# Half steps in lockstep, 128-column pieces of maxima and masks off TensorE in the two 16-head attentions

## What is computed

```python
# l2a: heads of 8 features, strict mask: masked scores are 0, not -inf
att = einsum('bhqe,bhke->bhqk', q, k) / sqrt(8)
att = softmax(att * tril(ones, k=-1), axis=-1)
out = einsum('bhqk,bhke->bhqe', att, v)          # then out @ Wr + br
# l2r: heads of 4 features, rotated q and k, causal mask
c = rmsnorm(x) @ w_down                          # 64 latents
q, k, v = rope(c @ wq), rope(c @ wk), c @ wv
scores = where(causal, q k^T / sqrt(4), -inf)
x = x + (softmax(scores) @ v) @ w_up
```

## Time and profile before

| | us |
|---|---|
| median of three runs (4970.01 to 4974.94) | 4973.66 |
| the profiled execution | 4970.81 |
| its span, first to last instruction | 4969.1 |
| PE busy | 3646.9 (73%) |
| DVE busy | 2768.8 (56%) |
| ACT busy | 1422.5 (29%) |
| POOL busy | 727.7 (15%) |
| mean granted TensorE clock, share of 2.4 GHz | 0.794 |

### The profile page before, as it was taken

How to read it: one execution, slowest core, us unless ns; L and a number is a source line. 1 busy time by engine, 2 the same in 40 slices (tenths; PEclk the granted TensorE clock), 3 DMA queues, 4 the chain that set the end, 5 groups by cost and what they waited for, 6 DMA issues and landing times. The chain is left out here.

```text
span 4969.1 us, 75102 instructions
## 1 busy us (share of the span) xinstructions
PE 3646.9 (73%) x29138; PEld 2469.8 (50%) x29138; DVE 2768.8 (56%) x7107; ACT 1422.5 (29%) x2785; POOL 727.7 (15%) x465
## 2 busy tenths in 40 slices
PE   4577887887548788778654878878865487887885
PEld 4354654455435455445443545544545355554454
DVE  6674544456576454445757655444575765444457
ACT  3033332320304333232130433323213133332320
POOL 2142200000114220000012332000001233200000
PEclk6588987898558888799755888878975598897897
DMA  1000000000000000000000000000000000000000
GB/s 25 5 19 19 1 2 2 12 16 1 6 11 13 19 1 2 2 11 17 1 6 23 1 19 1 2 1 11 17 1 6 23 1 19 1 2 1 11 17 5
DMA packets 55964, 43.16 MB, mean 9 GB/s; under 512 B 14451, under 2 KB 52262, under 8 KB 55590
## 3 DMA queue, kind: packets, MB, share of 16 engines
q1 hardware_dynamic: 54358, 37.53, 2.6%
q10 hardware_dynamic: 1232, 0.61, 0.1%
HBM read 35.50 MB, written 2.10 MB: 8 GB/s over the span
## 5 line engine op out<-in xcount | busy, mean ns | idle before, releaser
L157 POOL TENSOR_TENSOR ln_rstd<-ln_var_eps,neghalf 128x4 f32<-128x4 f32 x128 | 129.8, 1015 | 2199.2 <-DVE ln_var_eps L169 2199.1
L1906 DVE TENSOR_REDUCE l2r_m<-l2r_bank_ring 128x1 f32<-128x384 f32 (+3 forms) x352 | 207.2, 637 | 259.8 <-PE l2r_bank_ring L1755 259.8
L1906 DVE TENSOR_REDUCE l2a_m<-l2a_bank_ring 128x1 f32<-128x384 f32 (+3 forms) x352 | 207.2, 637 | 247.5 <-PE l2a_bank_ring L1755 247.5
L1137 POOL TENSOR_TENSOR l1t_ss<-l1t_ss,neghalf 128x16 f32<-128x16 f32 x64 | 240.4, 3756 | 460.0 <-DVE l1t_ss L1192 460.0
L2020 ACT ACTIVATE l2r_P<-l2r_bank_score 128x512 f32<-128x512 f32 x320 | 168.6, 594 | 284.7 <-PE l2r_bank_score L1782 156.5
L2020 ACT ACTIVATE l2a_P<-l2a_bank_score 128x512 f32<-128x512 f32 x320 | 169.3, 597 | 268.3 <-PE l2a_bank_score L1782 140.0
L1381 PE MATMUL l1t_ring<-l1f_qkv,x_normT 128*128 128x512 f32 x384 | 226.8, 741 | 13.5 <-ACT x_normT L1046 13.5
L1746 PE MATMUL l2r_bank_ring<-l2r_k_head,l2r_q_head 32*128 32x256 f32 (+3 forms) x1024 | 184.2, 540 | 33.5 <-DVE l2r_m L1906 26.8
L1465 PE MATMUL l1t_score<-l1t_q_head,l1t_k 128*128 128x256 f32 (+1 forms) x896 | 207.2, 363 | 0.0
L1746 PE MATMUL l2a_bank_ring<-l2a_k_head,l2a_q_head 32*128 32x256 f32 (+3 forms) x1024 | 176.6, 516 | 25.8 <-DVE l2a_m L1906 21.8
L1346 ACT ACTIVATE l1t_P<-l1t_score 128x512 f32<-128x512 f32 x176 | 105.2, 598 | 222.9 <-PE l1t_score L1465 222.9
(11 more groups left out here) (561 smaller groups left out, 8483.2 us busy)
## 6 DMA issues: line engine op xcount, KB each, us to landing
l2e_w<-in_L_ffn_w SPq DMA_DIRECT2D x96, 128.0 KB, 2.2
l1f_qkv<-in_L_ffn_wqkv SPq DMA_DIRECT2D x8, 768.0 KB, 4.3
l1f_tables<-in_l_tables SPq DMA_DIRECT2D x8, 512.0 KB, 5.9
l1f_w<-in_L_ffn_w SPq DMA_DIRECT2D x8, 341.0 KB
x_in<-in_L_attn_hidden_states SPq DMA_DIRECT2D x10, 256.0 KB, 3.5
l1f_wo<-in_L_ffn_wo SPq DMA_DIRECT2D x8, 256.0 KB, 4.6
l2a_q_head<-l2a_shiftT SPq DMA_DIRECT2D x128, 2.0 KB
l2r_q_head<-l2r_shiftT SPq DMA_DIRECT2D x128, 2.0 KB
```

Source lines behind the costliest of these rows:

```text
L157: pool.tensor_tensor(b.rs[:, p, :], b.ve[:, p, :], b.neghalf[:, 0:NT], ALU.pow).then_inc(s["post_rstd"] if post else s["pre_rstd"], 1)
L1137: pool.tensor_tensor(ss[:, n % 2], ss[:, n % 2], b.neghalf[:, 0:2 * H8], ALU.pow).then_inc(s["rn_ready"], 1)
L1906: dve.tensor_reduce(self.m[:, n, 4 * g + u:4 * g + u + hb], bank, AX, ALU.max).then_inc(s["max_ready"], 1)
```

## The change

All of it is in `Attention16` and the two stages that use it.

- Steps become 40 half steps h: an even one handles the score products of row groups 0 and 1, an odd one those of 2 and 3 (`pe_half`). Beside them, two by two, PE makes 128-column pieces of two units of maxima of the other two row groups. There are at most two units in a half (`beside`), 28 such pairs; 12 pairs that don't fit stand alone behind the values (`extra`).
- The values of half h-2 follow the scores of half h (`PV_LAG` = 2).
- The score masks are no longer added by PE: GpSimd's `affine_select` sets the masked part of `P` to zero behind the exponential on the diagonal steps, four per tile, and the values wait for it (`p_masked`).
- The masks of the maxima of one-head units (64 of 88) are no longer added by PE: DVE adds a table `neg_wide` and takes the maximum in one `tensor_tensor_reduce`, which also writes the masked scores as bf16. Units of 4 and 2 heads stay as they were.
- The turns stand at planned halves (`turn_at`). The lead-in is put in another order: key heads of both sequences and the first maxima come ahead of the values' products; in l2r the two sequences' projections have banks of their own.
- Eight bf16 products of 512 columns (`pe_filler`, `KICK` = 8), whose result is overwritten, stand ahead of the loop; inside it there are none (`KEEP` = 0).
- The projection moves into the end of the loop: seven of its eight blocks stand ahead of the last half's values. The post norm of sequence 0 comes ahead of the last tile's division. The biases of l2a are laid out as 512 columns and added by one product for a sequence instead of four.

```diff
-    RING, CHUNK, P_RING = 3, 3, 8
+    RING, P_RING, PV_LAG, KICK, KEEP = 3, 8, 2, 8, 0
...
+        self.wide = sb("neg_wide", [128, S])
+        self.masked = sb("masked", [128, 4, S], BF16)
...
+        for n in range(2, len(self.tiles)):
+            end = max(begin + 2, 2 * self.first[n] - (2 if n < 5 else 3))
+            heads = range(0, 4, self.PER_BANK[self.tiles[n][0]])
+            left = {pair: [[(g, u) for g in pair] for u in heads] for pair in ((2, 3), (0, 1))}
+            order, total = [], 2 * len(heads)
+            for h in range(begin, end):
+                due = (h + 1 - begin) * total // (end - begin) - len(order) // 2
+                for nth in range(due):
+                    pair = ((2, 3), (0, 1))[(h + nth) % 2]
+                    pair = pair if left[pair] else pair[::-1] if left.get(pair[::-1]) else ((0, 1) if pair == (2, 3) else (2, 3))
+                    fits = pair != self.groups(h) and not self.beside[h]
+                    units = [(n, len(order) + i) for i in range(2)]
+                    order += left[pair].pop(0)
+                    (self.beside if fits else self.extra)[h].extend(units)
+            self.units[n] = order
+            self.turn_at[end].append(("shift", n, "shiftT_ready"))
+            begin = end
+        for n in range(len(self.tiles)):
+            last = 2 * self.first[n + 1] - 1 + self.PV_LAG
+            self.turn_at[last + 1].append(("token", n, self.token_read))
+            self.turn_at[last + 3].append(("oT", n, "oT_ready"))
...
+    def pe_half(self, pe, h):
+
+        units = self.beside[h]
+        for i, g in enumerate(self.groups(h)):
+            if h >= 2:
+                pe.wait_ge(self.s["p_ready"], 2 * (h - 2) + i + 1)
+        self.pe_filler(pe, self.s_bank[self.groups(h)[0]], self.KEEP)
+        views = [self.max_view(pe, *unit) for unit in units]
+        for r in range(4):
+            for unit, view in zip(units, views):
+                self.pe_max_piece(pe, *unit, view, r)
+            self.pe_scores(pe, h, r)
+        self.pe_max_mask(pe, units, views)
...
+            if kt == self.tiles[n][0]:
+                pe.wait_ge(s["p_masked"], 4 * n + g + 1)
+            else:
+                pe.wait_ge(s["p_ready"], 4 * k + g + 1)
...
+        pe.matmul(self.o_bank[:, :], b.ident_bf[0:1, :], b.zero_row[:], start=True, stop=True)
+        self.pe_filler(pe, self.s_bank[0], self.KICK)
...
+        for h in range(len(self.turn_at)):
+            if h < self.halves:
+                self.pe_half(pe, h)
+            if 0 <= h - self.PV_LAG < self.halves:
+                self.pe_values(pe, h - self.PV_LAG)
+            if h < self.halves:
+                self.pe_extra(pe, h)
+            if h == self.halves:
+                project(pe, 0, 0, NT)
+                project(pe, 1, 0, NT - 1)
+            for kind, n, _ in self.turn_at[h]:
+                turn[kind](pe, n)
+        project(pe, 1, NT - 1, NT)
...
+                P = self.P[:, (4 * k + g) % self.P_RING]
+                pool.affine_select(out=P, in_=P, compare_op=ALU.is_gt if self.strict else ALU.is_ge, fill=0.0, base=0,
+                                   pattern=[[0, 4], [1, 128]], channel_multiplier=-1).then_inc(s["p_masked"], 1)
...
-            dve.tensor_reduce(self.m[:, n, 4 * g + u:4 * g + u + hb], bank, AX, ALU.max).then_inc(s["max_ready"], 1)
+            into = self.m[:, n, 4 * g + u:4 * g + u + hb]
+            if hb == 1:
+                use = self.m_first[n] + i
+                dve.wait_ge(s["max_ready"], use - 3)
+                ins = dve.tensor_tensor_reduce(self.masked[:, use % 4, 0:N], bank[:, 0, :], self.wide[:, S - N:], 1.0, MASKED,
+                                               ALU.add, ALU.max, into)
+            else:
+                ins = dve.tensor_reduce(into, bank, AX, ALU.max)
+            ins.then_inc(s["max_ready"], 1)
...
-            post_norm(dve, step, b, s, at.y)
+            post_stats(dve, step, b, s, at.y, 0)
+            at.dve_finish(dve, step, len(at.tiles) - 1)
+            post_apply(dve, step, b, s, at.y, 0)
+            post_stats(dve, step, b, s, at.y, 1)
+            post_apply(dve, step, b, s, at.y, 1)
```

More of the change, by code:

```diff
@@ L1788, in pe_values, with pe_extra @@
+    def pe_extra(self, pe, h):
+        for i in range(0, len(self.extra[h]), 2):
+            units = self.extra[h][i:i + 2]
+            views = [self.max_view(pe, *unit) for unit in units]
+            for r in range(4):
+                for unit, view in zip(units, views):
+                    self.pe_max_piece(pe, *unit, view, r)
+            self.pe_max_mask(pe, units, views)
+    def pe_values(self, pe, h):
+        s, k = self.s, h // 2
+        n, kt = self.steps[k]
         p = self.tiles[n][1]
-        if kt == 0 and n:
+        if kt == 0 and n and h % 2 == 0:
@@ L1790, in pe_values @@
             pe.wait_ge(s["sums_ready"], n)
[L1791 to L1792 removed]
+        for g in self.groups(h):
+            if kt == self.tiles[n][0]:
+                pe.wait_ge(s["p_masked"], 4 * n + g + 1)
+            else:
+                pe.wait_ge(s["p_ready"], 4 * k + g + 1)
             for c in range(4):
@@ L1797, in pe_values @@
             last.then_inc(s["pv_done"], 1)
-    def pe_turns(self, pe, k):
-        for kind, n, _ in self.turns(k):
-            {"shift": self.pe_shift, "token": self.pe_token, "oT": self.pe_turn}[kind](pe, n)
     def pe_shift(self, pe, n):
@@ L2025, in act @@
-        for k in range(len(self.steps), len(self.steps) + 3):
-            self.act_turns(act, k)
-            self.act_sums(act, k)
+        for h in range(len(self.turn_at)):
+            if h < self.halves:
+                for i, g in enumerate(self.groups(h)):
+                    use = 2 * h + i
+                    act.wait_ge(s["s_ready"], use + 1)
+                    if use >= self.P_RING:
+                        act.wait_ge(s["pv_done"], use - self.P_RING + 1)
+                    act.activation(self.P[:, use % self.P_RING].rearrange("k h q -> k (h q)"), self.s_bank[g][:, :],
+                                   ACT.Exp, scale=self.scale).then_inc(s["p_ready"], 1)
+            n = self.ended(h)
+            if n is not None:
+                self.act_sums(act, n)
+            for kind, n, _ in self.turn_at[h]:
+                if kind == "shift":
+                    self.act_shift(act, n)
+                elif kind == "oT":
+                    self.act_turn(act, n)
```

370 lines of the change are left out of this document (179 added, 191 removed).

## The result

The changed kernel takes 4786.39 us (median of four runs, 4784.68 to 4792.11), the kernel before 4973.34 (4970.01 to 4974.94): a ratio of 0.9627, with a 95% interval of 0.961 to 0.9644.

What follows compares the result with a forecast made beforehand. PE, busy 84% but taking turns with DVE at clock 0.92, was the engine to look at. Loops 3.5 and 5.1 plus tails 6.3 gain 14.9 us a round, four rounds 60: 4914 us, range 4825 to 5025.

Steps and rivals of the forecast that it cites:

- the chain over DVE: Paired halves: pieces end at 1.04 us, DVE's first reduction 0.85, next bank claim 0.1 later; 2.0 a half with N=512.
- the clock: In each loop: 30 us at the lower clock, so 10 us lost; bounds none and 70.
- The loop's sum at 2.4 GHz: Halves, lone pairs, turns and a wait for rows make 111.8 us a loop, against 125.3 and 126.9 before.
- The halves without maxima: 12 halves of each loop with scores and values only: 1.8 us of PE each.
- A lone pair with no partner: In the loop: a pair standing alone costs PE as much as a full lockstep; twelve take 22.0 us.
- The turns: In the loop: 7 of sums at 0.66 us, 13 of shifts and results at 0.30, each plus 0.17 for a layout change: 11.9.
- falls and stays down: Rival, chance 0.17: last 12 halves, lone pairs and start run at 1.2 GHz, about 70 us a loop; 5020 us in all.
- Lead-in of l2a: Ahead of l2a's loop: reordering gives back 2 us at most, fillers add about 2.1; put at 0, plus or minus 3.
- Tails: Behind the loops: moving the projection forward saves 5 us in l2a and 1.3 in l2r, 6.3 a round.
- GpSimd's masks: Selects on diagonal steps, 0.8 to 1.7 us each, hidden before the values: cost nothing, at the bad end 16 us an execution.
- The rival on DVE: Rival, chance 0.06: the fused reduction takes as long as the scan, 1.219 us; 5074 in all, deciding from about 0.97 each.
- The warm rival: Rival, chance 0.22: the clock stays up, each loop takes 111.8 us, the kernel 4834.

Runs made afterwards that it cites:

- `KICK` = 0: The changed kernel without the eight bf16 filler products ahead of either loop: 4775.45 us.

## Why the prediction was wrong

The direction was right, and so was the chain over DVE in the paired halves; three terms were wrong, all to the same side, and one of them, the clock, also in its mechanism.

**The loop's sum at 2.4 GHz: 111.8 forecast, 105.0 measured** (the l2a loop at clock 1.00 above; no l2r loop of any run was free of low clock), 6.8 a loop, 54 us if both stages are taken alike. In that loop (first round, `KICK` = 0) the halves begin at 650.85, 670.76, 693.63, 701.08 and 736.77 for these groups; the forecast's terms, added up for the same halves with their lone pairs and turns (and the 0.9 for the first rows):

| halves | with | forecast | measured |
|---|---|---|---|
| 0 to 5 | N=256, 2 lone pairs | 20.4 | 19.91 |
| 6 to 12 | N=384, 5 lone pairs | 24.4 | 22.87 |
| 13 and 14 | 3 lone pairs in succession | 9.4 | 7.45 |
| 15 to 28 | N=512, 2 lone pairs | 36.0 | 35.69 |
| 29 to 39 | no maxima | 21.6 | 19.08 |

The prices of paired halves and of single lone pairs were right: a half with N=512 takes 2.01 (2.0), and with a lone pair behind the values halves take 4.51, 3.34 and 4.01 for N=256, 384 and 512 (4.5, 3.4 and 4.0). Three steps failed.

*The halves without maxima, 1.8 forecast, 1.64 measured.* Scores and values of such a half, and the next scores:

```profile
742.51 1.16 PE L1803 MATMUL l2a_bank_score<-l2a_q_head,l2a_k_head 32*128 32x128 f32 x16 [0.53 <-DMA l2a_q_head<-l2a_shiftT]
743.60 0.62 PE L1850 MATMUL l2a_bank_o<-l2a_P,l2a_v_head 128*9 128x128 f32 x16
744.16 0.38 PE L1803 MATMUL l2a_bank_score<-l2a_q_head,l2a_k_head 32*128 32x128 f32 x2
```

From start to start 1.09 and 0.56, both changes of layout included, where 1.0, 0.6 and 0.2 for the changes had been put down. That is 1.6 in ten halves. The last half was counted whole (1.8), though the loop as measured ends with its scores (0.89). The wait for rows is here (0.53, tile 7's), not at the start.

*A lone pair with no partner, 9.4 forecast for halves 13 and 14, 7.45 measured.* The forecast let each pair behind the values stand alone. Behind half 13, which takes 1.98 instead of 3.4, comes one without maxima. Its scores need no bank of the ring and wait for no maximum: they start 0.34 behind the lone pair's first pieces and run beside them, in the other two row groups:

```profile
695.28 0.60 PE L1771 MATMUL l2a_bank_ring<-l2a_k_head,l2a_q_head 32*128 32x128 f32 x6
695.62 0.38 PE L1803 MATMUL l2a_bank_score<-l2a_q_head,l2a_k_head 32*128 32x128 f32 x2
695.71 0.38 PE L1771 MATMUL l2a_bank_ring<-l2a_k_head,l2a_q_head 32*128 32x128 f32 x3
```

*The turns, each with a change that nothing overlaps.* Where two or three fall into one half of the N=384 group they cost less: half 6 takes 4.31 instead of 5.17, half 10 2.57 instead of 3.0.

**The clock: 30 us low forecast, 8.5 and 11.1 measured.** A third of the difference, 7 and 6 us a loop, is 54 us. (The third is right: an l2a loop takes 105.0 with no low clock, 106.4 with 3.4 us and 108.9 with 13.7.) The term was a choice between 0 and 70 made by counting parts that "use two row groups". The trace after has no fall in the last eleven halves, which use two row groups only, nor has any other kernel here that alternates. The step that failed is that half-used row groups bring the clock down. What the runs show in its place: the falls come at the start of the loop, where N=256 halves wait, and in four of the eight loops behind half 14, where two lone pairs stand (3.4 us, from 706.8 on), and with alternation each is over within 10.3 us. What starts a fall stays open. The rival "falls and stays down" (0.17) had a state that exists: the kernel without alternation is in it, at 5326. But it looked for it in the lone pairs and the last halves of this kernel, where it is not.

**Lead-in of l2a: 0 forecast, -5.9 measured**, 24 us in all. The step was "PE busy 31.6 of 33.5, so reordering gives back 2 at most". Busy was taken for necessary. The layout of the biases was named in the change and then costed at nothing, with PE's occupancy as the reason; the rows of the alternating bias and weight products (0.42 each, start to start) were not read, though they are the same form as those of the tail. For l2r the lead-in was +2.4, of which the fillers are 3.7; there 0 was too low, since fillers were priced at 2.1 for eight, at 2.4 GHz.

**Tails**: -6.6 and -1.9 against -5 and -1.3, 9 us in all. The mechanism was right (undoing the projection's place and the bias layout costs what was expected).

Together 54 + 54 + 24 - 10 + 9 = 131, against 128 between forecast and result. The large errors were all to one side; where errors cancelled, in the parts of the N=512 chain, it was luck that the half came out at 2.0.

**GpSimd's masks** were rightly costed at nothing, with 0.63 us each instead of the 0.8 to 1.7 considered. They cost DVE a little. Its product of two SBUF operands (L2002) takes 0.30 us by the median, as before, but 0.76 in one tile of each l2a loop, where a select of GpSimd had just begun:

```profile
693.29 1.29 POOL L1959 TENSOR_SCALAR_AFFINE_SELECT l2a_P<-l2a_P 128x512 f32<-128x512 f32 x2 [9.30 <-ACT l2a_P L2090]
...
693.32 0.76 DVE L2002 TENSOR_TENSOR l2a_acc<-l2a_suffix,l2a_e 128x144 f32<-128x144 f32 x1
```

That is 0.46 more, four times in the kernel, 2 us at most. The rule of the Trainium skill that the prediction weighed (SBUF — State Buffer, "SBUF: two separate sides") says that such a pair of instructions shuts each other out for a whole one. This row agrees in kind, with 0.46 of the 0.6 that the select still had to go, and with the masks back on PE no such row is longer than 0.31.

**The rival on DVE** fell: 0.77 with the read-out, even without their overlap, below the 0.97 from which it decides.

**The warm rival** was nearest, 4834. It kept the 111.8. With 105.0, a clock at 1.00 in all loops would come to some 4761 (eight loops of 105.0 instead of 107.7 and 108.6).

**The range** failed because its lower end was the warm rival with the same sum: the terms of the sum had been taken as certain, and only the clock as uncertain.

## What to carry to other kernels

When a loop's granted clock has two levels, ask not only what makes it fall but whether the loop's own order lets it return; compare rounds of one execution that differ in nothing else. Busy time is no floor: small products of different shapes that alternate can be busy for half as long again as the same columns need in a row (3.3 us against 2.1). A mask that an idle engine can add, or that a reduction takes with it, is worth taking off the engine that is waited for, even without any other change.

## What the hardware showed that was not expected

- The same loop of products took 160.2 us at a clock of 0.60 and 108.1 at 0.98 in two rounds of one execution, PE busy for over 90% in both. A busy PE does not by itself bring the clock back: in blocks of two row groups 15 of 16 loops stayed low for 129 us or more; alternating products of four row groups were back within 10.3 us, with two bf16 fillers of 512 columns a half the loops were back within 28.
- An fp32 product of one row and 128 columns that alternates with one of 128 rows takes 0.42 us from start to start at 2.4 GHz, each; in a row four of the latter take 1.09.
- The fused add and maximum of 512 columns costs 0.689, the plain maximum 0.686: the second operand is free there. Its read-out is a separate 0.083, which overlaps the next one (0.62 from start to start).
- A half of pieces and scores takes 1.65 us when they alternate and 2.20 when they stand in blocks, both at 2.4 GHz with DVE out of the way.
- An edit in one stage moved the low clock of another, untouched one: l2r's loop took 2.7 us more when l2a's biases were laid out anew.
